# A graph network on one core: consumers a slot or more behind their producers, segment flags kept as bytes in SBUF, one table stored instead of two

## The reference

```python
x = _layernorm(x + _L0_gnn_ref(x, edge_index, W, att, bias))        # GAT with 4 heads
x = _layernorm(x + _L1_gnn_ref(x, Wq, Wk, Wv, Wo, edge_index))      # attention over a node's edges
x = _layernorm(x + _L2_gnn_ref(x, edge_index, W0, b0, W1, b1))      # two GCN layers, relu
x = _layernorm(x + _L3_gnn_ref(x, edge_attr_3, edge_weight, ...))   # messages with a radial net
...
# _L1: numer = segment_sum(w[:, None] * V[sender], receiver); return x + (numer / denom) @ Wo
# _gcn_layer: h = x @ W; out = segment_sum(h[src] * (dinv[dst] * dinv[src])[:, None], dst); return out + b
# _L2: x = relu(_gcn_layer(x, ..., W0, b0)); x = relu(_gcn_layer(x, ..., W1, b1))
# _L3: gather up-projected senders, form 8 x 32 message columns, segment_sum by receiver, project, / 16
```

## Time and profile before

| what | value |
| --- | --- |
| three runs | 7854.48, 7871.08, 7896.73 us; median 7871.08 |
| the profiled execution | 7874.37 us, its span 7872.4 us |
| busy share of the span | PE 51%, PEld 40%, DVE 45%, ACT 34%, POOL 48% |
| mean granted TensorE clock | 0.672 |
| DMA | 1048.5 MB, mean 133 GB/s |
| one flags load (an item) | 256.0 KB |

### The profile page before, as it was taken

One profiled execution on the slowest core, in us unless ns is written; L12 is line 12 of the kernel. 1 busy time (PEld: TensorE's weight loads), 2 busy tenths in 40 slices (PEclk: granted clock), 3 DMA queues, 4 the chain that ended last, 5 costly groups with the idle time before them and its releaser, 6 DMA issues. The chain is left out here.

```text
span 7872.4 us, 85274 instructions
## 1 busy us (share of the span) xinstructions
PE 4003.5 (51%) x18822; PEld 3174.7 (40%) x18822; DVE 3570.1 (45%) x12700; ACT 2687.6 (34%) x6766; POOL 3751.2 (48%) x4124
## 2 busy tenths in 40 slices
PE   2444444112961118825468764444556885555555
PEld 1443344101641015514356543333554554555554
DVE  4484444001671005548711135553334665656665
ACT  0014455001861018815433324442222332222222
POOL 3655655775006750003255532225665664666665
PEclk9655555555985559957789975556666666777676
DMA  1236666111851016624455547776777996333333
GB/s 51 64 89 184 185 191 188 36 19 48 262 174 34 21 39 216 216 64 132 110 132 151 158 129 193 190 192 155 178 180 183 220 218 150 98 101 98 101 98 79
DMA packets 1395766, 1048.50 MB, mean 133 GB/s; under 512 B 171017, under 2 KB 1232586, under 8 KB 1395521
## 3 DMA queue, kind: packets, MB, share of 16 engines
q1 hardware_dynamic: 1279294, 866.89, 39.6%
q0 software_dynamic: 112896, 179.36, 10.1%
q10 hardware_dynamic: 3458, 1.02, 0.1%
HBM read 603.60 MB, written 448.78 MB: 134 GB/s over the span
## 5 line engine op out<-in xcount | busy, mean ns | idle before, releaser
L985 POOL DMA_INDIRECT t_alpha<-gsm_raw,gsm_edge_idx x392 | 401.8, 1025 | 591.7 <-DVE gsm_raw L1107 467.2
L1128 PE MATMUL gsm_zr<-kept_ident,gsm_zT 128*128 128x128 f32 x784 | 141.0, 307 | 936.8 <-ACT gsm_zT L1030 749.4
L1952 POOL DMA_INDIRECT out_dram<-mss_o,kept_scat_idx x392 | 390.8, 997 | 364.6 <-ACT mss_o L1297 274.0
L511 POOL DMA_INDIRECT sort_xd<-in_x_dram,kept_dst_idx x392 | 378.6, 966 | 382.9 <-DMA t_xdst<-sort_xd 226.6
L1417 POOL DMA_INDIRECT asc_xs<-t_t,kept_idx_a x392 | 370.8, 946 | 354.2 <-issue 120.3
L1336 POOL TENSOR_TENSOR l_xb<-l_x,kept_bias 128x512 f32<-128x512 f32 x98 | 133.5, 1363 | 842.0 <-DMA l_x<-t_xdst 841.3
L741 PE MATMUL sort_sps<-kept_wa,sort_xdT 128*128 128x4 f32 x784 | 221.6, 353 | 607.0 <-ACT sort_xsT L765 572.8
L1128 PEld LDWEIGHTS gsm_zr<-kept_ident,gsm_zT 128*128 128x128 f32 x784 | 89.8, 150 | 986.9 <-ACT gsm_zT L1030 797.3
L1822 POOL DMA_INDIRECT gs_xs<-t_z,kept_idx_a x392 | 370.7, 946 | 237.0 <-issue 94.0
L1724 POOL DMA_INDIRECT gs_xs<-t_t,kept_idx_b x392 | 370.7, 946 | 214.6 <-issue 105.8
L978 POOL DMA_INDIRECT gsm_raw<-t_al,gsm_from_idx x392 | 395.6, 1009 | 161.5 <-issue 129.1
(11 more groups left out here) (527 smaller groups left out, 12860.5 us busy)
## 6 DMA issues: line engine op xcount, KB each, us to landing
t_t<-sort_o SPq DMA_DIRECT2D x66, 792.0 KB
t_x<-gsm_o SPq DMA_DIRECT2D x196, 264.0 KB
sort_x<-in_x_dram SPq DMA_DIRECT2D x66, 768.0 KB
gsm_x<-t_t SPq DMA_DIRECT2D x196, 256.0 KB
t_z<-gsm_z SPq DMA_DIRECT2D x196, 256.0 KB
out_dram<-gsm_o SPq DMA_DIRECT2D x196, 256.0 KB
gs_cont<-t_cont SPq DMA_DIRECT2D x196, 256.0 KB
t_t<-l_o SPq DMA_DIRECT2D x98, 264.0 KB
```

The source lines that it names most:

```text
L511: pool.indirect_dma_start(xd[u][:, j, :], None, A["x"], bass.IndirectOffsetOnAxis(K["dst_idx"][:, c:c + 1], 0)).then_inc(gathered[u], 16)
L985: pool.indirect_dma_start(T["alpha"], bass.IndirectOffsetOnAxis(edge_idx[:, c:c + 1], 0), raw[:, c, :], None).then_inc(scattered[u], 16)
L1952: pool.indirect_dma_start(T["out"], bass.IndirectOffsetOnAxis(K["scat_idx"][:, c:c + 1], 0), o[u][:, j, :], None, bounds_check=N - 1, oob_ ...
```

## The change

Lags grow in the four stages, and some parts change their order within a slot. The flags are written as bytes, loaded once to all partitions in radial_basis (128 x 50,176 bytes, K["cont"]) and read there by the scans. The radial net's tiles are freed behind attention_scores to make room. `second_layer` stores z alone; `gcn_second` loads z as its x, scales the relu by 1/degree in a new ACT step `lift`, and adds in SBUF, which gives the old sum times 1/sqrt(degree); the norm takes that out, with `degepsB` now eps/degree.

```diff
-SCATTER_LAG = 4
+SCATTER_LAG = 13
...
-def edge_line(table, t, u):
-    return table[0:1, bass.ds(t * (4 * BUFS * P) + u * 4 * P, 4 * P)].broadcast_to([P, 4 * P])
+def goes_on(K, t, u):
+    return K["cont"][:, bass.ds(t * (4 * BUFS * P) + u * 4 * P, 4 * P)]
...
 prepare
-            dve.tensor_tensor(same[0:rows], cur[0:rows], nxt[0:rows], ALU.is_equal).then_inc(same_ready, 1)
+            link(dve.tensor_tensor(same[0:rows], cur[0:rows], nxt[0:rows], ALU.is_equal))
+            dve.tensor_copy(same8[0:rows], same[0:rows]).then_inc(same_ready, 1)
...
 gat_sums
-            link(dve.tensor_scalar(K["degepsB"][:], K["totB"][:, HEADS, :], 1.0, EPS * D, ALU.add, ALU.mult))
+            link(dve.tensor_tensor(K["dinv2B"][:], K["dinvB"][:], K["dinvB"][:], ALU.mult))
+            link(dve.tensor_scalar(K["degepsB"][:], K["dinv2B"][:], EPS * D, None, ALU.mult))
...
 radial_basis, SP, between the loads of r and of the weights
+            sp.dma_start(K["cont"][:], T["cont"][0:1, 0:EP].broadcast_to([P, EP])).then_inc(cont_loaded, 16)
...
 second_layer
-                wait_item(sp, scanned, t, u, 4)
-                wait_item(sp, summed, t, u, 4)
-                sp.dma_start(xs[u][:], edge_rows(T["xsrc"], t, u)).then_inc(xs_loaded[u], 16)
-                sp.dma_start(cont[u][:], edge_line(T["cont"], t, u)).then_inc(cont_loaded[u], 16)
+                sp.dma_start(xs[u][:], edge_rows(T["xsrc"], t, u)).then_inc(xs_loaded[u], 16)
+
+            def load_own(t, u):
+                wait_item(sp, summed, t, u, 4)
...
-                sp.dma_start(edge_rows(T["x2"], t, u), o2[u][:]).then_inc(x_stored[u], 16)
-            pipeline(sp, (load, 0), (store, 5))
+            pipeline(sp, (load_xs, 0), (load_own, 3), (store, 10))
...
-                pool.tensor_tensor(rsx[u][:], norm["rs"][u][:], four(K["dsqrtB"], t, u), ALU.mult)
-                pool.tensor_tensor(nbx[u][:], norm["nb"][u][:], four(K["dsqrtB"], t, u), ALU.mult).then_inc(widened[u], 1)
-            pipeline(pool, (widen, 3), (weight, 0))
+            pipeline(pool, (weight, 0), (widen, 6))
...
-            pipeline(pe, (multiply, 1), (turn, 0))
+            pipeline(pe, (multiply, 3), (turn, 1))
...
-                    ac = act.activation(o2[u][:, j, :], y[u][:, j, :], ACT.Identity, bias=nbx[u][:, j:j + 1], scale=rsx[u][:, j:j + 1])
-            pipeline(act, (apply, 4), (lambda t, u: norm_root(norm, act, t, u), 3))
+            pipeline(act, (lambda t, u: norm_root(norm, act, t, u), 5), (apply, 7))
...
-                dve.tensor_tensor_scan(sc[u][:], cont[u][:], tp[u % 2][:].rearrange("p j i -> p (j i)"),
+                dve.tensor_tensor_scan(sc[u][:], goes_on(K, t, u), tp[u % 2][:].rearrange("p j i -> p (j i)"),
-            pipeline(dve, (scan, 0), (add, 1), (scale, 2))
+            pipeline(dve, (scan, 2), (add, 4), (scale, 5))
...
 gcn_first: no flags load
-            pipeline(sp, (load, 0), (store, 3))
+            pipeline(sp, (load, 0), (store, 7))
-            pipeline(pe, (multiply, 1), (turn, 0))
+            pipeline(pe, (multiply, 2), (turn, 0))
-            pipeline(act, (activate, 2))
+            pipeline(act, (activate, 4))
-            pipeline(dve, (scan, 0), (take, 1))
+            pipeline(dve, (scan, 1), (take, 3))
...
 gcn_second: no flags load
-                sp.dma_start(x2[u][:], edge_rows(T["x2"], t, u)).then_inc(x_loaded[u], 16)
+                sp.dma_start(x2[u][:], edge_rows(T["t12"][T12_Z:T12_Z + EP], t, u)[:, :, 0:D]).then_inc(x_loaded[u], 16)
-            pipeline(sp, (load, 0), (store, 4))
+            pipeline(sp, (load_own, 0), (load_root, 1), (load_x, 3), (store, 9))
-                wait_item(pe, summed, t, u, 2)
+                wait_item(pe, lifted, t, u, 2)
-            pipeline(pe, (multiply, 1), (turn, 0))
+            pipeline(pe, (multiply, 2), (turn, 0))
+            def lift(t, u):
+                act.wait_ge(multiplied[u], t + 1)
+                wait_item(act, summed, t, u, 4)
+                for j in range(4):
+                    ac = act.activation(r[u][:, j, :], hp[u % 2][:, j, :], ACT.Relu, scale=K["dinv2B"][:, bass.ds(4 * BUFS * t + 4 * u + j, 1)])
+                ac.then_inc(lifted[u], 1)
-            pipeline(act, (lambda t, u: norm_apply(norm, act, t, u, stored), 3), (lambda t, u: norm_root(norm, act, t, u, bias=K["zero"]), 2))
+            pipeline(act, (lambda t, u: norm_root(norm, act, t, u, bias=K["zero"]), 5), (lift, 3), (lambda t, u: norm_apply(norm, act, t, u, stored), 6))
-                dve.scalar_tensor_tensor(out=y[u][:], in0=hp[u % 2][:], scalar=0.0, in1=x2[u][:],
-                                         op0=ALU.max, op1=ALU.add).then_inc(summed[u], 1)
+                dve.tensor_tensor(y[u][:], r[u][:], x2[u][:], ALU.add).then_inc(summed[u], 1)
-            pipeline(dve, (scan, 0), (add, 1), (lambda t, u: norm_scale(norm, dve, t, u), 2))
+            pipeline(dve, (scan, 1), (add, 4), (lambda t, u: norm_scale(norm, dve, t, u), 5))
...
 final_edges: no flags load
-            pipeline(sp, (load, 0), (load_y, 2))
+            pipeline(sp, (load, 0), (load_y, 5))
-            pipeline(pe, (reduce, 2), (turn_sums, 1), (turn_x, 0), (project, 0))
+            pipeline(pe, (turn_x, 1), (reduce, 7), (project, 3), (turn_sums, 5))
-            pipeline(act, (lambda t, u: norm_apply(norm, act, t, u, scattered, 64), 4), (lambda t, u: norm_root(norm, act, t, u), 3),
-                     (scale_x, 0), (copy_x, 0))
+            pipeline(act, (copy_x, 2), (lambda t, u: norm_root(norm, act, t, u), 9), (scale_x, 0),
+                     (lambda t, u: norm_apply(norm, act, t, u, scattered, 64), 10))
-            pipeline(dve, (scan, 1), (messages, 0), (combine, 2), (lambda t, u: norm_scale(norm, dve, t, u), 3))
+            pipeline(dve, (scan, 6), (messages, 4), (combine, 8), (lambda t, u: norm_scale(norm, dve, t, u), 9))
```

More of the change, by code:

```diff
@@ L1588, in second_layer @@
         own = [sb(f"own{u}", [P, 4, D]) for u in range(BUFS)]
-        cont = [sb(f"cont{u}", [P, 4 * P]) for u in range(BUFS)]
         sc = [sb(f"sc{u}", [P, 4 * P]) for u in range(BUFS)]
@@ L1800, in gcn_second @@
         x2 = [sb(f"x2{u}", [P, 4, D]) for u in range(BUFS)]
-        cont = [sb(f"cont{u}", [P, 4 * P]) for u in range(BUFS)]
+        r = [sb(f"r{u}", [P, 4, D]) for u in range(BUFS)]
         root = [sb(f"root{u}", [4, P]) for u in range(BUFS)]
```

70 lines of the change are left out of this document (34 added, 36 removed).

## The result

The changed kernel takes 7648.2 us (median of 4 runs, 7635.3 to 7666.0), the kernel before beside it 7880.4 us (4 runs): ratio 0.971, 95% interval 0.9675 to 0.9745. That is faster, but by 3% where the forecast of 7235 us said 8%, and outside the range. Later runs on other chips gave 0.91. The prediction rested on a trace of an L chip.

The account below looks back on a forecast made before the run. Engines waiting for one another within a slot were taken to bound aggregation and final_edges, transfers gcn_second. Gains of 262 + 82 + 79 + 224 = 647 us less 7 us added, from 7874.4, gave 7235 us; range 7150 to 7460.

Parts of the forecast that it names:

- Part 1: Aggregation (second_layer): with the new lags DVE becomes the bound at 4.1 us a slot, 427 instead of 689.5 us, -262 us.
- the lock: DVE's two-input SBUF operations held up beside POOL's products; up to 5.05 us an aggregation slot; as a growing rival 7387, chance 0.12.
- Part 2: gcn_first: lags remove POOL's waiting for transposes, leaving its 5.0 us gather floor a slot; 515 us, -82 us.
- Part 3: gcn_second: flags load gone, lift hidden beside POOL, 5.2 us a slot between POOL's 5.0 and PE's 5.5; 540 us, -79 us.
- that stage is bound by transfers: gcn_second before the change: DMA engines busy 0.95 of the time at 218 GB/s, so transfers bound it.
- The rival with transfers at gcn_first's 174 GB/s: Transfers hold the convolutions back: gcn_first gains nothing (+79), aggregation needs 4.6 us a slot (+49); 7363 us, chance 0.10.
- The price of the add: gcn_second: DVE's add with two SBUF inputs contends with GpSimd, putting a slot nearer 5.5 than 5.0 us.
- Part 4: final_edges: scatters 13 slots behind gathers find rows ready, POOL needs 10.5 us a slot; 1056 us, -224 us.
- One stage does not come apart: Rival: most dearly final_edges, its y load waiting for ACT's last step of an older slot, stays at 1280; 7459, chance 0.08.
- The closed ring: Rival in final_edges: waits over four buffers make engines work in turn, 18.5 us a slot, 1816 us; total 7995, chance 0.03.
- the byte flags: Rival: scans with byte flags take twice their 1.28 us, aggregation 5.4 us a slot (+127); 7365 us, chance 0.03.
- No stretch read here moves half of it: Argument against the transfer rival: no stretch moved half of the fabric's 435 GB/s in the mean.

Follow-up runs that it names:

- L chip: A chip of the kind on which the kernel before takes 7825 to 7883 us; a chip kind, not a run.
- P chip: A chip of the kind on which the kernel before takes 6387 to 6393 us; a chip kind, not a run.
- run 6: The kernel before, unedited, traced on a P chip: 6388 us, with gcn_second 556.2 and final_edges 1274.2 us.
- run 5: The changed kernel, unedited, on a P chip: 5819 us beside 6393 for the kernel before.
- run 11: Changed kernel with gathers of gcn_first and final_edges as plain loads of consecutive rows on SP, on an L chip: 6859 us, those stages 341.7 and 840.4.
- run 1: Changed kernel with final_edges back to its old order and scatter lag 4, flags still bytes, on a P chip: 6091 us, final_edges 1273.3.
- run 15: Changed kernel with gcn_second's lifted rows written to PSUM instead of SBUF, three rounds on a P chip: 5806.8 us against 6389.6, ratio 0.9088.
- run 13: Changed kernel with POOL's lead in final_edges cut to two slots (scatter lag 11) and gcn_second's lifted rows in PSUM, on a P chip: 5814 us.
- run 8: Changed kernel with gcn_second's lifted rows written to PSUM instead of SBUF, on an L chip: 7586 us, gcn_second 604.7.

## Why the prediction was wrong

Measured gains in us, against its own terms:

| term | forecast | L chip | P chip |
|---|---|---|---|
| second_layer | 262 | 287.5 | 286.3 |
| gcn_first | 82 | 7.3 | 0.5 |
| gcn_second | 79 | 5.2 | 28.9 |
| final_edges | 224 | -58.9 | 255.5 |
| radial_basis | -5 | -2.2 | -2.1 |

- **Part 1 was right and 25 us too careful.** A slot takes 3.92 us (3.91 in the mean of all), not 4.1; the lock that was to cost up to 0.3 us does not show.
- **The step that failed is the reading of POOL's idle time in Part 2: "The rest of POOL's slot is waiting", and with it that a gather's wait for "the transposes four slots back" is one that lags shorten.** That was right of the time and wrong of its cause. On a P chip gcn_first has no such wait before the change; its floor of 490 + 25 = 515 us was sound (504.8), but the kernel before stands on it there already. On an L chip 106 of the 115 us that POOL stands between slots fall behind transposes that had ended: TensorE's late signals. The new lags do not take them away: 111 us of them and 590.5 us with the change.
- **Part 3 fell by the same step.** 527.3 us on a P chip are below the 540 forecast; the gain is 28.9, as the stage took 556.2 there. What was forecast does happen in it: POOL waited 50.0 us for TensorE's transposes before (run 6) and waits for nothing after. On an L chip 5.2 us are left of the gain. The sentence "that stage is bound by transfers" holds in so far as DMA is busy 0.93 at 233 GB/s in it on a P chip. The rival with transfers at gcn_first's 174 GB/s falls: that rate was the stage's need, not a limit (205 GB/s in the same stage in run 6). The price of the add, weighed but not taken into the sum, is 11.5 us of the stage.
- **Part 4's mechanism is shown on P chips**: POOL waits for ACT hardly at all, and a scatter lag of 11 suffices. 1018.7 us against 1056. A lag of 10 was run on an L chip alone, where it costs 182 us or more (1499.8). On L chips the forecast that rows are ready 13 slots later fails: POOL waits 251 of 1100 us for ACT, which waits for TensorE's signals. The kernel before hardly pays there (1280.9 and 1274.2); its POOL pauses in nearly each slot (93 of 96 stretches are of 8 transfers, with a pause of 2.4 us in the median behind them). That these pauses let the signals through would explain it, but was not tried.
- **The rivals.** "One stage does not come apart" named final_edges and 7459, for its y load; the stage did stay on the L chips (1317 to 1352 us and not the 1056 forecast), for a cause outside it. The closed ring falls with runs 5 and 11, the byte flags with runs 1 and 11. "No stretch read here moves half of it" is not so of the earlier trace rows, whose 218 GB/s are half of the fabric's figure, and the ring outweighs the gains from 17.3 us a slot on, not 17.1; neither moves the sum. No rival named a signal that comes late, though the earlier trace rows carries "remote 24.6" and "remote 10.1" and I passed over both.

On a P chip the sum comes to 569 us between the spans of runs 6 and 5 (6385.9 and 5816.6), where 640 were forecast: too small gains in the convolutions, somewhat larger ones in the other two stages.

A version with a shorter gcn_second on P chips is that of run 15: 515.8 us there and in run 13, where all runs without the edit have 525.4 or more. As a whole it can't be told from the changed kernel: ratio 0.9088 (0.9073 to 0.9104) beside 0.9102 of run 5, on another chip. On L chips its run 8 gave 7586 beside 7825, ratio 0.969, the changed kernel's too.

## What to carry to other kernels

Before an idle stretch is put down to the order of the work, take one of its waits and compare when the producer ended with when the waiter started: here 17 us lay between them, and none of the lags tried took them away. A releaser named "remote", or a DMA of an earlier stage, is a reason to look: here such rows were those waits. Floors by busy time told the times of the changed stages within 7% on chips with prompt signals; what they did not tell was whether the kernel before stood on that floor already, and for that its own time per slot has to be explained, not only undercut.

## What the runs showed of the hardware

- Of the five chips met after the result, two have TensorE's signals arrive late beside indirect transfers from POOL, three have not; the chip of the result is of the first kind and may be one of the two. The same kernel takes 7825 to 7883 us on the one kind and 6387 to 6393 on the other, and the ratio of the two kernels is 0.97 or 0.91. What differs in the chips, and on what path the signal is held, no run here shows; nor does one part indirect issue from scattered rows.
- Late are TensorE's signals; DVE's and ACT's, in the stall shown, stand 0.01 to 0.02 us behind their instructions, and TensorE's steps start at most 0.1 us behind what they need. DVE waits up to 2.4 us for the steps of its own norm a few times on the L chip (9.5 us in all before L1294 in final_edges) and never in run 5, so its signals to itself may be late too. Plain transfers issued by POOL do not bring it (243.5 and 244.0 us on the two kinds of chip).
- A plain load that POOL issues takes it 0.546 us, one by index 0.944 with 0.30 behind it; on P chips gcn_first is 244 us with the one and 505 with the other.
- A gather by index takes 944 ns, and 1045 in the mean beside a DVE add of 512 columns with both inputs in SBUF (run 5); with one input in PSUM it stays at 944 (run 15).
